# A graph, attention and product-key-memory block on one core: edge additions issued pair by pair, a shorter front, statistics taken per tile, and memory rows gathered as four slots of 32 tokens

## The chip, the cores and the metric

The kernel runs on one core of a Trainium2 chip, in one launch. The metric is the device time in microseconds, the median of the timed runs. Everything is float32.

## What is computed

For 1250 nodes of 512 features (`x`) and 20000 edges:

```python
xn = layernorm(x)
x = x + gnn(xn, src, dst, edge_type)      # two relational layers, 30 bases each
      + mix(xn)                           # two blocks: linear attention with 256 random features, then an MLP
# the memory, on y = layernorm(x):
q = (y @ Wq + bq).reshape(-1, 8, 128)     # 8 heads, two halves of 64
s1t, i1 = top_k(q1 @ keys1, 8)            # 256 keys for each half
s2t, i2 = top_k(q2 @ keys2, 8)
scores, best = top_k(s1t[:, None] + s2t[None, :], 8)
rows = i1 * 256 + i2                      # at best: 64 rows a token
out = x + sum_k relu(y . w_down[rows]) * softmax(scores) * w_up[rows]
```

The graph sum over edges is done as a product with a dense adjacency matrix (2 x 1250 x 1250 counts in DRAM).

## The kernel before

The 1250 tokens are ten tiles of 125 tokens, handled in five pairs where a stage works on 250 columns. All five engine programs are written out by hand, with semaphores between them. What stands first in a program runs first on that engine, and an engine waits in order. The stages:

1. **Front.** SP (SyncE's queue) loads `x`, the edges, then every weight of the first attention block (`attn_loads_sp`): three matrices, seven short vectors whose elements are scattered (L415), two broadcast vectors, the projection. Only then come the edge cells' way through DRAM (L303, L304, and L306, which spreads them over all partitions, 10 MB), the write of the normalised `x` (L309) and the zeroing of two adjacency copies (L314, 25 MB). DVE computes the cells, the statistics and norm of `x` (L344 to L352), and then the same statistics again for the attention block's own norm (`ln1_dve`, L445).
2. **Attention, block 0** (`attn1_*` to `attn3_*`). Beside the keys of each pair, `merge_dve` compares the edges' cells with each other, to merge repeated edges (32 of 160 groups a pair). After the last pair `edge_index_dve` makes all 160 groups' indices, and only then GpSimd (POOL) starts its 160 indirect additions into the adjacency copies (`adjacency_pool`, L285), followed by ten DMAs that add one copy to the other (L292). Behind them on POOL's queue stand the 60 loads of half a basis each for graph layer 2 (`half_bases_pool`, L1085).
3. **MLP of block 0** (`mlp_*`), opened by `ln2_dve`: statistics of all ten tiles (L829), then the norm. Beside it DVE combines the bases of graph layer 1, which SP loads (L434).
4. **Graph layers** (`gcn_*`), with the half bases combined on DVE (L1097) ahead of each tile's `xroot` addition (L1109).
5. **Attention, block 1**, and again `ln2_dve`.
6. **Memory and the second MLP** (`mem_*`), the last 1.1 ms. The MLP is cut into halves of a pair; half g runs beside tile g-3. For each tile of tokens, `front` on PE makes the queries (L1241) and scores (L1253), `top` on DVE searches them, and POOL gathers 64 times 128 rows of 4 KB (a down row and an up row) into a ring of 8 buffers (L1210), one gather for each slot: partition p holds token p. `dot` on DVE (L1538) multiplies the down half by the token and sums; ACT turns the 125 sums into a diagonal matrix of 125 x 125 (L1385); PE multiplies that matrix by the up half and adds into bank 7 (L1304). The buffer is then free, and POOL, which waits for `p_up`, may issue the next gather into it. `TURN_AT`, `QUERY_AT`, `SCORE_AT`, `HALF_AT`, `SEARCH_AT` and `TAIL_AT` say behind which slot's row each piece of other work stands in PE's, ACT's and DVE's programs. `take` (L1546) moves a finished tile out of bank 7.

The four lines of a slot:

```python
nc.gpsimd.indirect_dma_start(out=ring[s % RING], ..., in_=a["L0_ffn_rows"], in_offset=...(ap=slots_of[t % 2][:, s:s + 1], axis=0))
nc.vector.scalar_tensor_tensor(ring[s % RING][0:P, 0:DIM], ring[...], probs_of[t % 2]...[:, s:s + 1], xl[:, t % 2, :], ALU.mult, ALU.mult, accum_out=inner[:, s:s + 1])
nc.scalar.activation(diags[:, s % DRING, :], ident[0:P, 0:P], ACT.Relu, scale=inner[:, s:s + 1])
nc.tensor.matmul(psum[7][0:P, :], diags[:, s % DRING, :], ring[s % RING][0:P, DIM:ROW], start=(s == 0), stop=(s == SLOTS - 1), ...)
```

## Time and profile before

| | |
|---|---|
| median of 3 runs | 2818.54 us (2815.58 to 2827.08) |
| the profiled execution's own time | 2807.37 us |
| its span | 2805.3 us |
| busy: PE, DVE, POOL, ACT | 91%, 53%, 37%, 25% |
| memory rows: first gather issued to last `take` | 1755.8 to 2800.2 us |
| moved by DMA | 524.29 MB, 380 MB of it by POOL's queue |

The profile is one execution. A float32 matmul of the program appears as two MATMUL records. Their ends are modelled and overlap, so what a matmul costs PE is read from the distance between starts. "issue" is time in which an engine waited for nothing that the profile shows.

### The profile page before, as it was taken

How to read it: one execution, taken by the hardware profiler on the slowest of the kernel's cores; microseconds unless marked ns; L12 is line 12 of the kernel's file. 1: busy time of each engine (PE TensorE's matmuls, PEld its weight loads, DVE VectorE, ACT ScalarE, POOL GpSimd, SP SyncE). 2: the span in 40 equal slices, each digit the busy share in tenths (PEclk: the TensorE clock that was granted, in tenths of full speed). 3: DMA queues.
4: the chain of work that ended last, by engine and by line, in shares of the span. 5: the costliest groups of instructions: out<-in, count | busy, mean ns of one | idle time of the engine just before them, and what ended most of it. 6: DMA issues, size and time to landing. Idle time of an engine off the chain costs nothing.

```text
span 2805.3 us, 25699 instructions
## 1 busy us (share of the span) xinstructions
PE 2551.7 (91%) x8620; PEld 1400.3 (50%) x8620; DVE 1479.4 (53%) x3776; ACT 707.5 (25%) x1651; POOL 1042.4 (37%) x887
## 2 busy tenths in 40 slices
PE   2999979999499999999999978999989989998877
PEld 2666656765244444445656656545445445443321
DVE  4665675455376500001335634577677677677664
ACT  0346231211010011001454311333323323322322
POOL 0005877774021100000000000566656656656665
PEclk9999989999799999999999989999999999999999
DMA  8924144548776520431005000889988988989998
GB/s 283 302 67 124 3 91 111 116 91 171 189 205 186 152 58 0 130 101 55 1 1 169 1 8 8 281 309 318 334 304 317 332 311 307 336 322 337 360 354 331
DMA packets 235961, 524.29 MB, mean 187 GB/s; under 512 B 99362, under 2 KB 99737, under 8 KB 231675
## 3 DMA queue, kind: packets, MB, share of 16 engines
q0 software_dynamic: 170032, 379.99, 41.7%
q1 hardware_dynamic: 63257, 137.66, 16.2%
q10 hardware_dynamic: 2550, 5.12, 0.5%
q8 instruction: 64, 1.05, 0.2%
q14 instruction: 58, 0.48, 0.0%
HBM read 489.51 MB, written 45.34 MB: 191 GB/s over the span
## 4 chain that ended last, share of the span: by engine, by line
PE 78%; DVE 10%; DMA 5%; issue 3%; another core or an unknown queue 2%; ACT 1%; POOL 1%; SPq 0%; POOLq 0%; DVEq 0%; ACTq 0%
PE bank L1304 13%; PE bank L1056 12%; PE bank L892 5%; PE bank L903 5%; PE bank L1284 5%; PE bank L1294 4%; PE bank L1033 4%; PE bank L668 3%; PE bank L560 3%; PE bank L774 3%; PE bank L1241 3%; PE bank L567 2%; PE bank L574 2%; PE bank L1043 2%; PE bank L600 2%
## 5 line engine op out<-in xcount | busy, mean ns | idle before, releaser
L1385 ACT ACTIVATE stage<-ident,qv 125x125 f32<-125x125 f32 x640 | 246.3, 398 | 513.9 <-DVE qv L1538 184.5
L1304 PE MATMUL bank<-qv,stage 125*125 125x512 f32 x640 | 338.9, 619 | 32.9 <-ACT stage L1385 16.1
L1538 DVE SCALAR_TENSOR_TENSOR qv<-qv 125x512 f32<-125x512 f32 x320 | 238.0, 750 | 150.6 <-DMA qv<-in_L_ffn_rows,biasb 71.2
L285 POOL DMA_INDIRECT adj<-e_cnt,e_idx x80 | 164.3, 2054 | 275.7 <-issue 238.0
L1204 POOL MEMSET wreg<- 64x2048 f32 x2 | 3.6, 1801 | 688.3 <-DVE h L699 688.2
L1210 POOL DMA_INDIRECT qv<-in_L_ffn_rows,qv x160 | 162.5, 1016 | 217.6 <-issue 140.2
L1304 PEld LDWEIGHTS bank<-qv,stage 125*125 125x125 f32 x640 | 111.1, 190 | 180.9 <-issue 113.6
L1210 POOL DMA_INDIRECT qv<-in_L_ffn_rows,biasb x160 | 161.3, 1008 | 99.8 <-PE bank L1304 71.4
L285 POOL DMA_INDIRECT adj_b<-e_cnt,e_idx x80 | 174.7, 2184 | 38.9 <-issue 26.2
L1304 PE MATMUL bank<-big,stage 125*125 125x512 f32 x320 | 166.8, 617 | 12.7 <-issue 6.5
L1056 PE MATMUL bank<-big,wreg 125*125 125x512 f32 x400 | 172.0, 592 | 0.0
L1056 PE MATMUL bank<-big,qv 125*125 125x512 f32 x400 | 171.8, 592 | 0.0
L1284 PE MATMUL bank<-stage,big 128*128 128x250 f32 x640 | 162.2, 379 | 4.9 <-ACT stage L1350 4.2
L1284 PEld LDWEIGHTS bank<-stage,big 128*128 128x128 f32 x640 | 122.7, 192 | 84.5 <-issue 68.1
L1294 PE MATMUL bank<-big 128*125 128x512 f32 x320 | 161.0, 592 | 0.0
L1538 DVE SCALAR_TENSOR_TENSOR big<-big,qv 125x512 f32<-125x512 f32 x160 | 120.0, 750 | 75.8 <-DMA big<-in_L_ffn_rows,biasb 34.8
L1033 PE MATMUL bank<-qv,stage 128*125 128x512 f32 x320 | 146.2, 601 | 0.0
L1117 DVE TENSOR_TENSOR big<-bank,big 125x512 f32<-125x512 f32 x20 | 13.8, 691 | 247.3 <-PE bank L1056 247.3
L892 PE MATMUL bank<-stage,big 128*128 128x250 f32 x640 | 139.4, 378 | 1.2 <-ACT stage L924 1.2
L865 DVE SCALAR_TENSOR_TENSOR qv<-wreg,att_b,qv 128x2048 f32<-128x2048 f32 x60 | 138.4, 2347 | 2.8
L1097 DVE SCALAR_TENSOR_TENSOR qv<-stage,att_b,qv 128x1024 f32<-128x1024 f32 x90 | 109.8, 1276 | 55.4 <-DMA stage<-in_L_gnn_basis 55.4
L903 PE MATMUL bank<-big 128*125 128x512 f32 x320 | 139.0, 592 | 0.0
(224 smaller groups left out, 4211.1 us busy)
## 6 DMA issues: line engine op xcount, KB each, us to landing
wreg<-in_L_gnn_basis SPq DMA_DIRECT2D x30, 1024.0 KB
stage<-in_L_gnn_basis POOLq DMA_DIRECT2D x45, 512.0 KB, 4.4
big<-in_L_mix_W SPq DMA_DIRECT2D x4, 4096.0 KB
adj<-adj_b POOLq DMA_DIRECT2D x9, 1328.1 KB, 41.2
adj<-wreg SPq DMA_DIRECT2D x5, 2187.5 KB
adj_b<-wreg SPq DMA_DIRECT2D x5, 2187.5 KB
wreg<-adj SPq DMA_DIRECT2D x10, 1093.8 KB
qv<-adj SPq DMA_DIRECT2D x10, 1093.8 KB
```

The source lines that it names most:

```text
L285: nc.gpsimd.indirect_dma_start(out=(adj, adj_b)[g % 2], out_offset=bass.IndirectOffsetOnAxis(ap=e_idx[:, g:g + 1], axis=0), in_=e_cnt[:, g ...
L865: nc.vector.scalar_tensor_tensor(wrel[:, 0, r, :], wreg[:, n % BRING, :], att_b[:, 0, ds(i * BLOCKS + (r * BASES + n), 1)], wrel[:, 0, r, ...
L892: mm = nc.tensor.matmul(psum[F1_BANKS[n % 4]][:, 0:PT], w1_sb[:, k, 128 * n:128 * n + 128], y_t[:, k, :], start=(k == 0), stop=(k == KC - 1))
L903: mm = nc.tensor.matmul(psum[5 + j][0:P, :], act_t[:, k % HH, P * j:P * j + P], w2_sb[:, k, :], start=(k == 0), stop=(k == HC - 1))
L1033: mm = nc.tensor.matmul(psum[2 + 3 * j + r][0:P, :], gx_t[:, j, P * k:P * k + P], wrel[:, gl, r, 512 * k:512 * k + 512], start=(k == 0), s ...
L1056: mm = nc.tensor.matmul(psum[AGG_BANKS[j]][0:P, :], slabs[gl][:, j, c, :], zrel[:, c, :], start=(c == 0), stop=(c == COLT - 1))
L1210: nc.gpsimd.indirect_dma_start(out=ring[s % RING], out_offset=None, in_=a["L0_ffn_rows"], in_offset=bass.IndirectOffsetOnAxis(ap=slots_of[ ...
L1284: mm = nc.tensor.matmul(psum[F_BANKS[n % 2]][:, 0:PT], w1_sb[:, k, 128 * n:128 * n + 128], y_t[:, k, :], start=(k == 0), stop=(k == KC - 1))
L1294: mm = nc.tensor.matmul(psum[5 + j][0:P, :], act_t[:, k % HH, P * j:P * j + P], w2_sb[:, k, :], start=(k == 0), stop=(k == HC - 1))
L1304: nc.tensor.matmul(psum[7][0:P, :], diags[:, s % DRING, :], ring[s % RING][0:P, DIM:ROW], start=(s == 0), stop=(s == SLOTS - 1), skip_grou ...
L1385: nc.scalar.activation(diags[:, s % DRING, :], ident[0:P, 0:P], ACT.Relu, scale=inner[:, s:s + 1]).then_inc(p_diag, 1)
L1538: nc.vector.scalar_tensor_tensor(ring[s % RING][0:P, 0:DIM], ring[s % RING][0:P, 0:DIM], probs_of[t % 2].rearrange("p h k -> p (h k)")[:, ...
```

## The change

**Additions behind each pair.** `edge_index_dve(dve, i)` makes the indices of pair i's 32 groups right after that pair's merges (on DVE behind kmax n = 7 in pair 0, n = 3 in the others). POOL waits for a pair's indices as it comes to them, so it can start once pair 0's are there and the zeroing has ended.

**Shorter front.** The vectors and broadcasts are issued by ACT (`setup_act`) instead of SP; `bn_stats` of `x` stands ahead of the cells; the attention block's own statistics are worked out from the first norm's by three small operations instead of ten `bn_stats` and ten `bn_aggr`.

**Statistics per tile.** `ln2_dve` loses its ten `bn_stats` and `bn_aggr`; `attn3_dve` does them tile by tile, two units behind each tile's residual. This holds for both blocks.

**Rows as four slots of 32 tokens.** A gather takes, for token group g = s % 4 (32 tokens), four slots at once: partition 32e + m holds slot 4(s // 4) + e of token 32g + m. The 64 gathers a tile and their bytes stay. The diagonal matrix becomes 128 x 32 (`wsel`), and a row's matmul writes 32 partitions of bank 7, in column group g of the array. PE issues them two at a time (`late`). New work for each tile: 32 matmuls of 16 columns that spread slots and probabilities over the partitions (`spread_slots`), 4 matmuls of 512 columns and 4 ACT copies that make four replicated tokens (`spread_x`, `xrep`), and two DVE copies of 128 x 64. Scores are two matmuls of 64 rows and 256 columns into banks 3 and 4, instead of one of 128 rows and 512 columns against padded keys. Both banks are used by every head, so a head's scores wait for the search of the head before; formerly heads alternated between the banks. The ring has 9 buffers, numbered through the tiles.

```diff
         def adjacency_pool(pool):
-            pool.wait_ge(s_idx, 4)
             pool.wait_ge(s_adjz, 5 * 64)
             for g in range(GROUPS):
+                if g % CHUNK == 0:
+                    pool.wait_ge(s_idx, 4 * (g // CHUNK) + 4)
...
+        def setup_act(act):
+            attn_vectors(act, 0)
+            act.dma_start(att_b[:, 0, :], ...)
+            act.dma_start(att_b[:, 1, :], ...)
...
             if l == 0:
-                ln1_dve(dve, 0)
+                nc.vector.tensor_tensor(rs[:, 2, :], rs[:, 0, :], rs[:, 0, :], ALU.mult).then_inc(m["stat"], 1)
+                nc.vector.memset(mv[:, :, 0:1].rearrange("p t o -> p (t o)"), 0.0).then_inc(m["stat"], 1)
+                nc.vector.tensor_tensor(mv[:, :, 1], mv[:, :, 1], rs[:, 2, :], ALU.mult).then_inc(m["stat"], 1)
+                rsqrt(dve, m["stat"], 3, mv[:, :, 1], 0, TILES)
...
+                    if l == 0 and n == (3 if i else 7):
+                        edge_index_dve(dve, i)
...
+                if n >= 12 and n % 4 == 0:
+                    nc.vector.bn_stats(st6[:, T, :], h[:, T, :]).then_inc(m["ln2"], 1)
+                if n >= 13 and n % 4 == 1:
+                    nc.vector.bn_aggr(mv[:, T, :], st6[:, T, :]).then_inc(m["ln2"], 1)
...
-        QUERY_AT = [1 + hh - hh // 2 for hh in range(PKH)]
-        SCORE_AT = [10 + 3 * hh for hh in range(PKH)]
-        SEARCH_AT = SCORE_AT[0] + 3
-        TAIL_AT = SEARCH_AT + 25
+        QUERY_AT = [4 + hh - hh // 2 for hh in range(PKH)]
+        SCORE_AT = [10 + 4 * hh for hh in range(PKH)]
+        SEARCH_AT = SCORE_AT[0] + 1
+        TAIL_AT = SEARCH_AT + 4 * PKH - 1
...
             def row(t, s):
+                g = s % 4
-                pe.wait_ge(p_diag, t * SLOTS + s + 1)
-                nc.tensor.matmul(psum[7][0:P, :], diags[:, s % DRING, :], ring[s % RING][0:P, DIM:ROW], start=(s == 0), stop=(s == SLOTS - 1),
+                nc.tensor.matmul(psum[7][WIDE * g:WIDE * g + WIDE, :], wsel[:, s % DRING, :], ring[place(t, s)][:, DIM:ROW], start=(s < 4), stop=(s >= SLOTS - 4),
                                  skip_group_check=True).then_inc(p_up, 1)
...
             def late(n):
-                if n >= 0:
+                if n >= 0 and n % 2:
+                    pe.wait_ge(p_diag, n + 1)
+                    row((n - 1) // SLOTS, (n - 1) % SLOTS)
                     row(n // SLOTS, n % SLOTS)
...
             for _ in third:
                 pass
+            for _ in behind(0):
+                pass
```

`behind(t)` is the two `spread_slots` and the first two `spread_x` of a tile. For tile 0 it stands behind `third`, what is left of MLP half 2; for the others it stands at slots 52, 53, 56 and 57 of the tile before (`SPREAD_AT`). POOL's wait for a tile's slots is now for the copy out of the bank.

PE's order where the first rows start. L1284 and L1294 are the first and second product of MLP half 2, L1233 and L1241 the token's transposes and queries. Before:

```order
L1284 MATMUL bank<-stage,big 128x250 x2
L1294 MATMUL bank<-big 125x512 x6
L1233 MATMUL bank<-ident,qv 128x125 x4
L1241 MATMUL bank<-qv,wreg 128x125 x4
L1304 MATMUL bank<-qv,stage 125x512
L1241 MATMUL bank<-qv,wreg 128x125 x8
```

After (L1305, L1315 the MLP half, L1343 `spread_slots`, L1338 `spread_x`, L1325 the rows, L1251 and L1259 transposes and queries):

```order
L1305 MATMUL bank<-stage,big 128x250 x2
L1315 MATMUL bank<-big 125x512 x6
L1343 MATMUL bank<-qv,stage 32x16 x32
L1338 MATMUL bank<-qv,stage 128x512 x4
L1325 MATMUL bank<-qv,stage 32x512 x2
L1251 MATMUL bank<-ident,qv 128x125 x4
```

The spreading of tile 0's slots, which the first gather needs, has come behind the whole MLP half.

PE's order in the middle of a tile with an MLP half. Before (L1253 a head's scores):

```order
L1284 MATMUL bank<-stage,big 128x250 x2
L1304 MATMUL bank<-qv,stage 125x512
L1284 MATMUL bank<-stage,big 128x250 x2
L1304 MATMUL bank<-qv,stage 125x512
L1253 MATMUL bank<-wreg,qv 125x512
L1304 MATMUL bank<-qv,stage 125x512
L1294 MATMUL bank<-big 125x512
L1304 MATMUL bank<-qv,stage 125x512
```

After (L1273 a head's scores):

```order
L1325 MATMUL bank<-big,stage 32x512 x2
L1315 MATMUL bank<-big 125x512
L1325 MATMUL bank<-qv,stage 32x512 x2
L1305 MATMUL bank<-stage,big 128x250 x2
L1273 MATMUL bank<-wreg,qv 125x256 x2
L1315 MATMUL bank<-big 125x512
L1325 MATMUL bank<-qv,stage 32x512 x2
```

A row stood alone between two pieces; now two rows, in neighbouring column groups, stand between every two pieces.

SP's order in the front. Before:

```order
L412 DMA wreg<-in_L_mix_Wv 128x4x512
L415 DMA cols<-in_L_mix_ln_g 128x4x1
L415 DMA cols<-in_L_mix_ln_b 128x4x1
L415 DMA cols<-in_L_mix_ln_g 128x4x1
L415 DMA cols<-in_L_mix_ln_b 128x4x1
L415 DMA cols<-in_L_mix_bq 128x4x1
L415 DMA cols<-in_L_mix_bk 128x4x1
L415 DMA cols<-in_L_mix_b 128x16x1
L417 DMA biasb<-in_L_mix_bv 125x512
L417 DMA biasb<-in_L_mix_bo 125x512
L420 DMA ctx_flat<-in_L_mix_proj 128x2x64 x2
L303 DMA cells_t<-qv 128x125
```

After:

```order
L297 DMA qv<-in_edge_type 125x160
L411 DMA wreg<-in_L_mix_Wq 128x4x512
L411 DMA wreg<-in_L_mix_Wk 128x4x512
L411 DMA wreg<-in_L_mix_Wv 128x4x512
L414 DMA ctx_flat<-in_L_mix_proj 128x2x64 x2
L300 DMA cells_t<-qv 128x125
```

Seven vectors, two broadcast biases and the two broadcasts of `att` (formerly ahead of the matrices) have left SP's queue for ACT's, where they stand first.

## Rows read from the trace of the kernel before

**Rows 1.** Page, part 2: busy tenths and GB/s in 40 slices of 70 us.
```profile
PE   2999979999499999999999978999989989998877
DMA  8924144548776520431005000889988988989998
GB/s 283 302 67 124 3 91 111 116 91 171 189 205 186 152 58 0 130 101 55 1 1 169 1 8 8 281 309 318 334 304 317 332 311 307 336 322 337 360 354 331
```

**Rows 2.** Windows, `take` to `take`: tiles 0, 1, 2, 7 and 9.
```profile
core 0: us, PE busy (x) PEld busy (x) DVE busy (x) ACT busy (x) POOL busy (x), PEclk, DMA share, GB/s
1755.80:1874.60 118.80, 111.20 (x346) 58.98 (x345) 79.18 (x255) 36.05 (x91) 72.67 (x71) 0.98 0.89 314
1874.60:1978.60 104.00, 100.97 (x318) 53.42 (x318) 70.51 (x221) 33.53 (x87) 62.91 (x64) 0.99 0.88 308
1978.60:2089.00 110.40, 101.48 (x310) 52.41 (x310) 77.31 (x250) 33.19 (x85) 64.78 (x65) 0.98 0.92 329
...
2517.80:2614.20 96.40, 81.74 (x214) 32.14 (x214) 69.05 (x219) 27.48 (x73) 64.34 (x64) 0.96 0.91 331
...
2710.50:2800.20 89.70, 71.06 (x128) 18.99 (x128) 47.84 (x128) 25.14 (x63) 57.40 (x58) 1.00 0.94 358
```

**Rows 3.** Timeline of PE: rows back to back, and eight query matmuls before a row.
```profile
1964.30 1.02 PE L1304 MATMUL bank<-stage 125*125 125x512 f32 x2
1965.16 1.88 PE L1304 MATMUL bank<-big,stage 125*125 125x512 f32 x4
...
1980.33 1.95 PE L1241 MATMUL bank<-qv,wreg 128*128 128x125 f32 x16
1982.11 1.02 PE L1304 MATMUL bank<-qv,stage 125*125 125x512 f32 x2
```

**Rows 4.** Timeline of the front: cells to all partitions, nine of ten second statistics, PE's start.
```profile
35.91 0.36 SPq L306 DMA_DIRECT2D big<-cells_t  x1
...
39.71 5.42 DVE L445 BATCH_NORM_STATS2 st<-h 125x6 f32<-125x512 f32 x9
...
50.72 1.93 PE L549 MATMUL bank<-ident,stage 125*128 125x125 f32 x8 [14.53 <-DVE stage L472]
```

**Rows 5.** Timeline of POOL: first of 160 additions, the sum after the last, the fifth half basis.
```profile
214.50 2.20 POOL L285 DMA_INDIRECT adj<-e_cnt,e_idx  x1 [210.66 <-issue]
...
661.14 9.42 POOL L292 DMA_DIRECT2D adj<-adj_b  x10 [3.60 <-DMA adj_b<-e_cnt,e_idx]
...
748.58 0.72 POOL L1085 DMA_DIRECT2D stage<-in_L_gnn_basis  x1 [75.05 <-DVE qv L1097]
```

**Rows 6.** Timeline of SP: the queue's next issue after the zeroing.
```profile
160.86 0.39 SPq L408 DMA_DIRECT2D wreg<-in_L_mix_Wo  x1
```

**Rows 7.** Timeline of DVE: last pair's products of the MLP, first half basis.
```profile
675.96 0.69 DVE L847 TENSOR_TENSOR h<-bank,h 125x512 f32<-125x512 f32 x1 [18.00 <-PE bank L903]
...
745.80 7.26 DVE L1097 SCALAR_TENSOR_TENSOR qv<-stage,att_b,qv 128x1024 f32<-128x1024 f32 x6 [50.98 <-DMA stage<-in_L_gnn_basis]
```

**Rows 8.** Waits from 684 to 770 us: who waited for whom, us, times, longest.
```profile
PE bank L1043 <- DVE big L1109: 19.7, 1, 19.7
...
PE bank L1010 <- DMA stage<-xn_d: 16.9, 1, 16.9
```

**Rows 9.** Groups by line: statistics of the second norm, twice ten tiles.
```profile
L829 DVE BATCH_NORM_STATS2 st<-h 125x6 f32<-125x512 f32 x20 | 12.1, 678 | 0.2
```

**Rows 10.** Timeline where the first rows start: a head's scores, the MLP half's end, the first gather.
```profile
1742.27 1.09 PE L1253 MATMUL bank<-wreg,qv 128*125 128x512 f32 x2 [0.50 <-DVE qv L1432]
...
1761.08 5.31 PE L1294 MATMUL bank<-big 128*125 128x512 f32 x12
...
1755.83 1.05 POOL L1210 DMA_INDIRECT qv<-in_L_ffn_rows,qv  x1 [113.97 <-issue]
```

**Rows 11.** Timeline of PE: eight matmuls in four column groups of 32, then full width.
```profile
111.33 1.05 PE L580 MATMUL bank<-stage,headsel 128*32 128x250 f32 x16
112.31 1.98 PE L600 MATMUL bank<-projbd,stage 128*125 128x512 f32 x4
```

More of the change, by code:

```diff
@@ L45 @@
 SLOTS = PKH * TOPK
-RING = 8
-ROUNDS = SLOTS // RING
+RING = 9
 DRING = 8
@@ L318, in setup_dve @@
         def setup_dve(dve):
+            dve.wait_ge(s_xin, 32)
+            for t in range(TILES):
+                nc.vector.bn_stats(st6[:, t, :], h[:, t, :]).then_inc(s_ln, 1)
             dve.wait_ge(s_edge, 48)
@@ L340, in setup_dve @@
             nc.vector.tensor_copy(cell_ts[0:GROUPS - 128, 1, :], psum[0][0:GROUPS - 128, 128:128 + P]).then_inc(s_cellsb, 1)
-            dve.wait_ge(s_xin, 32)
-            for t in range(TILES):
-                nc.vector.bn_stats(st6[:, t, :], h[:, t, :]).then_inc(s_ln, 1)
             dve.wait_ge(s_ln, TILES)
@@ L699, in residual @@
                 nc.vector.tensor_tensor(h[:, T, :], h[:, T, :], b_o, ALU.add).then_inc(m["hat"], 1)
-            for n in range(UNITS + 7):
+            for n in range(UNITS + 10):
                 if n < UNITS:
@@ L827, in ln2_dve @@
             n = l * ADDS["ln2"]
-            for t in range(TILES):
-                nc.vector.bn_stats(st6[:, t, :], h[:, t, :]).then_inc(m["ln2"], 1)
-            dve.wait_ge(m["ln2"], n + TILES)
-            for t in range(TILES):
-                nc.vector.bn_aggr(mv[:, t, :], st6[:, t, :]).then_inc(m["ln2"], 1)
             dve.wait_ge(m["ln2"], n + 2 * TILES)
@@ L1202, in mem_pool @@
             pool.wait_ge(m["hat"], ADDS["hat"] + 2 + 2 * TILES)
[L1203 to L1204 removed]
             for t in range(TILES):
[L1206 removed]
+                pool.wait_ge(p_slots, 2 * t + 1)
                 for s in range(SLOTS):
@@ L1248, in front @@
                     pe.wait_ge(p_q, t * PKH + hh + 1)
-                    if hh >= 2:
-                        pe.wait_ge(p_top, t * TOPN + 4 * (hh - 1))
+                    if hh:
+                        pe.wait_ge(p_top, t * TOPN + 4 * hh)
                     elif t:
-                        pe.wait_ge(p_top, (t - 1) * TOPN + 4 * (PKH - 1 + hh))
-                    nc.tensor.matmul(psum[3 + hh % 2][0:P, :], pq_t[:, hh, :], keybd[:, hh, :], start=True, stop=True).then_inc(p_s_pe, 1)
+                        pe.wait_ge(p_xr, 4 * t)
+                    for s in range(2):
+                        rows = slice(64 * s, 64 * s + 64)
+                        mm = nc.tensor.matmul(psum[3 + s][0:P, 0:NKEYS], pq_t[rows, hh, :], keys_t[rows, hh, :], start=True, stop=True)
+                    mm.then_inc(p_s_pe, 1)
                     yield
@@ L1321, in mem_pe @@
                 pass
+            pe.wait_ge(p_sel, 2)
+            for _ in behind(0):
+                pass
             for t in range(TILES):
                 ahead = front(t + 1) if t + 1 < TILES else iter(())
+                found = behind(t + 1) if t + 1 < TILES else iter(())
                 beside = half(half_of(t)) if half_of(t) else iter(())
                 for s in range(SLOTS):
+                    if s == 0:
+                        spread_x(t, 2)
+                        spread_x(t, 3)
+                    for _ in range(SPREAD_AT.count(s)):
+                        next(found, None)
                     for _ in range((s == TURN_AT) + QUERY_AT.count(s) + SCORE_AT.count(s)):
@@ L1340, in mem_act @@
             act.wait_ge(p_w, 32)
-            for s in range(2):
-                for b in range(4):
-                    rows = slice(64 * s, 64 * s + 64)
-                    nc.scalar.activation(keybd[rows, 2 * b:2 * b + 2, NKEYS * s:NKEYS * s + NKEYS],
-                                         psum[2 + b][rows, :].rearrange("p (h m) -> p h m", h=2), ACT.Copy).then_inc(p_keysS, 1)
+            for b in range(4):
+                nc.scalar.activation(keys_t[:, 2 * b:2 * b + 2, :], psum[2 + b][:, :].rearrange("p (h m) -> p h m", h=2), ACT.Copy).then_inc(p_keysS, 1)
             def scale(i):
```

202 lines of the change are left out of this document (125 added, 77 removed).

## The prediction

> **What bounds the kernel now.** I read the page's slices first [rows 1]: PE is busy nearly throughout, so whatever shortens PE's path counts, except in two places: slices 1 and 11 (PE 2 and 4 tenths), and the last fifteen, where DMA is as full as PE. I went to each with the timeline or the waits.
>
> *Memory stage* (1755.8 to 2800.2, 1044.4 us). The windows go from one `take` to the next [rows 2]. Tile 9, with neither search nor MLP half beside it, takes 89.7 us for 64 gathers, 1.40 us each. PE has little to do there; this I take as the gathers' own pace. Tile 7 (search, no half) takes 96.4, tile 1 (a half too) 104.0, tile 2 (also `finish`, DVE's additions and statistics for the next pair) 110.4. PE's need comes from starts [rows 3]: a row of 512 columns 0.86 us, eight query matmuls 1.78. A tile with a half needs 64 x 0.86 = 55.0 for rows, 4 x 1.78 = 7.1 for queries, 8 x 0.86 = 6.9 for scores, 0.9 for transposes, and 32 pieces of 0.86, 27.5, for the half: 97.4 of tile 1's 104.0. Tile 7 needs 69.9 of 96.4. So PE bounds tiles 0 to 6, and DMA with lumps of PE and DVE the rest; busy time misleads, being modelled.
>
> *Front*: PE starts at 50.72, waiting for DVE, which takes the same statistics twice [rows 4].
>
> *Graph layer 1*: POOL starts its additions at 214.50 and the sum at 661.14 [rows 5], although the zeroing had ended by 160.86 [rows 6]. The half bases stand behind the sum: DVE waits 50.98 us for them, from 694.8 to 745.80 [rows 7], and POOL's fifth load waits for DVE [rows 5]. PE waits 19.7 for DVE, and 16.9 more for a 250 KB load that runs beside the sum [rows 8].
>
> **The change, part by part** (us against the profiled execution).
>
> *Front: -8.* Ten `bn_stats` and ten `bn_aggr` (nine of the former are 5.42) [rows 4] give way to three small operations: -6. The first statistics move ahead of the cells, and the cells no longer queue behind eleven DMAs on SP, which could give up to 6 more. Against it, DMA is full here [rows 1], and ACT's scattered elements now compete with `x` and the edges from the start. I count 2. Ends -3 and -12.
>
> *Indices beside the pairs: +1.* Six short DVE operations behind each pair; PE's turns of the next pair cover them. If not, +3.
>
> *Statistics per tile: -9.* Ten at 0.60 and ten `bn_aggr` leave the path in each block, 6.8 [rows 9]; the last tile's own stay, 0.8, and the second block gets a 125 x 512 copy (0.9) and a reduction. That is -11; I give back 2 for DVE's extra 0.7 us a tile in `attn3`. Ends -5 and -12.
>
> *Additions earlier: -34.* Start and sum move from 214.5 to about 158, now bound by the zeroing: 56 us. The half bases then land near 690. DVE, some 14 us earlier by the terms above, wants them near 681, and PE needs DVE's result only two tiles later. Both PE stalls, 16.9 + 19.7 [rows 8], should go, with 2 us of slower matmuls behind them; I leave 5 for the remaining wait. What is late next is PE itself. Ends -39 and -1 (below).
>
> *Start of the rows: +20.* Before, the first gather goes out at 1755.83, while PE works on MLP half 2 until 1766.4 [rows 10]. Now slots go through PE behind that half. Also each head's scores wait for the previous search: formerly a head took 1.09 + 0.50 = 1.59 [rows 10], set by DVE; in series it is 1.6 of search plus 0.65 to 1.09 of scores, I take 2.5, times seven heads: +6.3. PE's half ends at 1772.7, 16 spreading matmuls take 2, the DVE copy with its semaphores 0.7: first gather at 1775.4. Ends +14 and +24. Nothing hides this, since everything after goes at the gathers' pace.
>
> *Rows in column groups: -90.* The nearest row for price is the diagonal sums [rows 11]: eight matmuls of 250 columns in four groups of 32 occupy PE for 0.98 us; one after the other they would take 8 x 0.42 = 3.3, four abreast 0.83. So a pair of rows costs 0.86 at least and 1.72 at most; I take 1.0, since the overlap there was nearly full, and 32 pairs cost 32, not 55. Added: 4 x 0.86 = 3.4 (`spread_x`) and 32 small matmuls, two records each at 0.98 / 16 = 0.06, 3.9. Need with a half: 97.4 - 23 + 7.3 = 81.7, under the gathers' 89.7. Scores stay at 6.9 (3.5 if the two row halves overlap). ACT's matrix, a quarter as wide, saves perhaps 0.2 us a slot off the path. DVE keeps its 70 to 77 us and gets 0.6.
> A tile then goes at 89.7 plus the ring's stalls. Eight query pieces (14 us on PE) still fall behind five slots, and DVE's tail of the search is as thick as before, so I stay nearer to tile 7 than to tile 9: 94 for odd tiles, 98 with `finish` (4 of its 6.4, the rest in slack), 93 for tiles 7 and 8, 89.7 for tile 9, 102 for tile 0 with 4 for its first landing. 102 + 3 x 94 + 3 x 98 + 186 + 89.7 = 954, against 1044.
>
> Sum: -8 + 1 - 9 - 34 + 20 - 90 = -120. 2807.4 - 120 = 2687; the median of the runs stands 11 above the profiled execution, so 2698.
>
> **The rivals.**
>
> *A: the gathers alone set the pace.* If the ninth buffer and a faster PE leave no stall, ten tiles take 897 + 4: 53 less, 2645. For it: tile 9. Against: lumps of PE and DVE remain. 0.17.
>
> *B: changing between full width and column groups costs.* PE now changes twice for each pair. Each change may wait until the array is empty; a matmul's tail beyond its pitch is about 0.2 us (four records last 1.98, at 0.43 each 1.72) [rows 11], so 32 x 0.4 = 13 us a tile. PE needs 94.7 with a half, and such tiles come to 101 and 105: 6 x 7 + 6 = 48 more, 2746. For it: pairs stand singly between full-width pieces. Against: 0.98 for eight matmuls leaves only 0.15 for both changes. 0.17.
> The Trainium skill says in "TensorEngine Tiling (Array Packing)", Key Properties, that a change of tiling mode drains TensorE while different tiles work in parallel. The trace agrees with the second; it has no case of the first that costs more than 0.15 us.
>
> *C: the sum collides with basis loads.* The sum, from 661 before, moves into the last pair of the MLP, where SP still loads three bases of 1 MB. A 250 KB load beside the sum held PE 16.9 us [rows 8]; three loads so held are 51, and DVE's slack there is 18.0 [rows 7]: 33 back, 2731. 0.14.
> The Trainium skill's "DMA: Bandwidth & Descriptors" (Queues, rings and completion order) has each engine go round its queues packet by packet, which by itself would leave a load about half the rate. Its estimate would be some 10 us a basis, inside the slack, and 2698 would stand. The trace's load went slower than that.
>
> *D: the groups don't overlap (slower).* Then a pair costs 1.72, the rows 55 again, and PE needs 104.7 with a half; at the ratio of tiles 1 and 2 that is 111 and 118. Over the forecast: 3 x 17 + 3 x 20, 20 in tile 0, 7 in tiles 7 and 8: 138, so 2836. It decides from 1.5 us a pair, where PE's need is 97.4 again. Against it stands [rows 11]; but there the matmuls are short and four abreast. That the change does not do what it says would be this. 0.06.
>
> **How the numbers follow.** The forecast has 0.46, A 0.17, B 0.17, C 0.14, D 0.06. A measurement of this kernel tells about 0.5% from no change, 14 us. All but D are faster by more; B and C together, with a bad front, come near the bound: faster 0.92, same 0.04, slower 0.04. The range goes from below A to B and C together: 2635 to 2775.
>
> **What would show it.** Right: pairs of rows some 1.0 us apart from the next piece; `take` to `take` 93 to 98 with DMA at 340 GB/s or more; POOL's first addition near 158, and no DVE wait of tens of us for half bases; first gather about 20 us later after the search than before. Wrong: full-width spacing of 0.86 between rows of a pair (D), idle PE of 0.2 us around each pair (B), DVE waiting for basis loads around 640 (C), odd tiles at 90 (A), or PE starting later than 46.

## The result, and the profile after

The changed kernel takes **2769.4 us** (median of four runs, 2756.6 to 2790.9), the kernel before 2819.2 beside it: a ratio of 0.985, 95% interval 0.982 to 0.988. That is 50 us, where the prediction had 121, but inside its range and on its side. The profiled execution is the fastest of the four, 2756.6 (span 2754.8), 51 under before's; granted clock 0.939, before 0.974.

The slices of the changed kernel, to be read against [rows 1]:

```profile
PE   3999989997999999999999987889879879875665
POOL 0066877760111000000000000566666656666665
PEclk9999999998999999999999998999999999987856
DMA  9934145478466601440005000799999989989998
```

PE is no longer full in the last sixteen slices, and at their end its granted clock falls too. So PE no longer fills the memory stage, as predicted. Yet the stage is little shorter. Windows from one `take` to the next, in the changed kernel; first tile 0 from its first dot product, then tiles 1, 2, 8 and 9:

```profile
core 0: us, PE busy (x) PEld busy (x) DVE busy (x) ACT busy (x) POOL busy (x), PEclk, DMA share, GB/s
1737.40:1843.70 106.30, 88.29 (x396) 34.43 (x396) 77.83 (x253) 30.87 (x90) 70.30 (x70) 0.92 0.95 340
1843.70:1946.50 102.80, 89.88 (x404) 35.66 (x404) 68.89 (x224) 31.78 (x92) 63.52 (x62) 0.93 0.89 318
1946.50:2048.70 102.20, 84.85 (x396) 33.08 (x396) 76.69 (x250) 30.55 (x89) 66.43 (x66) 0.97 0.96 349
2559.80:2658.00 98.20, 66.41 (x300) 20.60 (x300) 68.06 (x220) 24.72 (x77) 66.27 (x64) 0.73 0.94 342
2658.00:2749.70 91.70, 53.64 (x128) 5.67 (x128) 47.92 (x128) 20.25 (x63) 56.38 (x58) 0.65 0.93 352
```

Against [rows 2], tile 1 lost 1.2 us and tile 2 8.2. The windows of tiles 3 to 7, cut in the same way, are 98.6, 105.0, 100.4, 104.9 and 102.2. Forecast were 94 for odd tiles, 98 for even ones, 93 for tiles 7 and 8. Tiles 1 to 8 are 4 to 9 us over their forecasts, 6.5 in the mean, whether an MLP half stands beside them (up to tile 6) or not.

The first gather goes out at 1733.0, before at 1755.8 [rows 10]; from there to the last `take` it is 1016.7 us, before 1044.4. So 28 us came from the row stage, and 23 from what lies ahead of it. Here are the changed kernel's PE at its start, POOL's first and last additions and the sum, two of DVE's three waits for a basis, and POOL's first gathers (timelines; where a line has "to", it gives minimum, median and maximum in ns and the first and last start):

```profile
41.94 1.93 PE L559 MATMUL bank<-ident,stage 125*128 125x125 f32 x8 [12.81 <-DVE stage L483]
...
L284 POOL DMA_INDIRECT adj<-e_cnt,e_idx x80: 1977/1982/3182, 156.7 to 586.2; - x80
...
595.41 9.42 POOL L291 DMA_DIRECT2D adj<-adj_b  x10 [4.36 <-DMA adj_b<-e_cnt,e_idx]
...
640.25 4.62 DVE L878 SCALAR_TENSOR_TENSOR qv<-wreg,att_b,qv 128x2048 f32<-128x2048 f32 x2 [10.86 <-DMA wreg<-in_L_gnn_basis]
654.88 4.61 DVE L878 SCALAR_TENSOR_TENSOR qv<-wreg,att_b,qv 128x2048 f32<-128x2048 f32 x2 [10.02 <-DMA wreg<-in_L_gnn_basis]
...
681.69 1.06 PE L1024 MATMUL bank<-ident,stage 125*128 125x125 f32 x4 [13.32 <-DMA stage<-xn_d]
...
686.75 7.26 DVE L1111 SCALAR_TENSOR_TENSOR qv<-stage,att_b,qv 128x1024 f32<-128x1024 f32 x6
...
L1228 POOL DMA_INDIRECT qv<-in_L_ffn_rows,qv x10: 936/937/1348, 1733.0 to 1754.0; - x10
```

PE starts 8.8 us earlier than in [rows 4]. The additions run from 156.7, and the 50.98 us wait for half bases of [rows 7] is gone. In its place DVE waits for the last three bases beside the sum, 10.9, 10.0 and 9.4 us, and PE 13.3 for the features, which stand behind the bases on SP's queue.

Who kept POOL waiting in the row stage? Its waits from 1740 us on, in the changed kernel (us in total, times, longest):

```profile
POOL qv L1228 <- issue: 87.6, 270, 1.0
POOL qv L1228 <- PE bank L1325: 85.2, 67, 3.8
POOL big L1228 <- PE bank L1325: 40.5, 26, 3.8
POOL big L1228 <- issue: 37.5, 110, 1.1
```

and of the kernel before, from 1755 on:

```profile
POOL qv L1210 <- PE bank L1304: 140.0, 154, 3.7
POOL big L1210 <- PE bank L1304: 68.4, 60, 6.4
```

With the two other regions of the ring, POOL waited 269 us for a buffer that PE had to free, and now 162; waits with no releaser in the profile ("remote") grew from 9 to 29. But a gather also costs POOL its own 1.01 to 1.03 us and, without any wait, a gap of 0.30 ("issue"). That is 1.31 us, 84 us a tile: a floor just under the 89.7 that I had taken for the transfers' pace.

### The profile page after: what moved, and what is told of

Its sections match the earlier page's. It is cut to its first block, busy times and chain, and to the rows that moved or that the text cites. A ratio compares the mean times of both kernels' runs of the same rounds, so it can differ in the third digit from the quotient of the medians.

```text
span 2754.8 us, 27581 instructions
## 1 busy us (share of the span) xinstructions
PE 2409.9 (87%) x9500; PEld 1234.4 (45%) x9500; DVE 1468.9 (53%) x3793; ACT 681.1 (25%) x1687; POOL 1036.3 (38%) x885
## 4 chain that ended last, share of the span: by engine, by line
PE 67%; DVE 13%; DMA 8%; issue 5%; POOL 3%; another core or an unknown queue 2%; ACT 1%; SPq 0%; DVEq 0%; POOLq 0%; ACTq 0%
PE bank L1070 12%; PE bank L1325 6%; PE bank L1047 5%; PE bank L905 4%; PE bank L916 4%; PE bank L1305 4%; PE bank L1315 3%; PE bank L1259 3%; PE bank L678 3%; PE bank L792 3%; PE bank L570 3%; PE bank L584 2%; PE bank L1057 2%; PE bank L577 2%; DMA qv<-in_L_ffn_rows,qv 2%
## 5 line engine op out<-in xcount | busy, mean ns | idle before, releaser
L1228 POOL DMA_INDIRECT qv<-in_L_ffn_rows,qv x356 | 360.1, 1012 | 1009.4 <-issue 909.0
L1448 ACT ACTIVATE stage<-stage,qv 128x32 f32<-128x32 f32 x640 | 200.3, 321 | 576.8 <-issue 199.0
L1325 PE MATMUL bank<-qv,stage 128*32 128x512 f32 x712 | 257.6, 699 | 91.6 <-ACT stage L1448 48.4
L1612 DVE SCALAR_TENSOR_TENSOR qv<-qv,wreg 128x512 f32<-128x512 f32 x356 | 262.8, 746 | 118.2 <-DMA qv<-in_L_ffn_rows,qv 98.0
L1305 PE MATMUL bank<-stage,big 128*128 128x250 f32 x640 | 174.2, 399 | 7.5 <-ACT stage L1407 7.5
L1228 POOL DMA_INDIRECT big<-in_L_ffn_rows,qv x142 | 145.8, 1027 | 88.1 <-PE bank L1325 40.5
L1315 PE MATMUL bank<-big 128*125 128x512 f32 x320 | 173.0, 633 | 2.1 <-issue 2.1
L1325 PE MATMUL bank<-big,stage 128*32 128x512 f32 x284 | 135.1, 722 | 35.9 <-ACT stage L1448 21.0
L1305 PEld LDWEIGHTS bank<-stage,big 128*128 128x128 f32 x640 | 115.6, 194 | 108.0 <-issue 91.1
L878 DVE SCALAR_TENSOR_TENSOR qv<-wreg,att_b,qv 128x2048 f32<-128x2048 f32 x60 | 138.4, 2348 | 32.9 <-DMA wreg<-in_L_gnn_basis 30.3
L1131 DVE TENSOR_TENSOR big<-bank,big 125x512 f32<-125x512 f32 x20 | 13.8, 692 | 247.2 <-PE bank L1070 247.2
L1612 DVE SCALAR_TENSOR_TENSOR big<-big,qv,wreg 128x512 f32<-128x512 f32 x142 | 105.4, 746 | 55.0 <-DMA big<-in_L_ffn_rows,qv 48.9
L905 PEld LDWEIGHTS bank<-stage,big 128*128 128x128 f32 x640 | 122.4, 192 | 20.1 <-issue 6.0
L1325 PEld LDWEIGHTS bank<-qv,stage 128*32 128x32 f32 x712 | 32.2, 115 | 213.3 <-ACT stage L1448 109.8
L1099 POOL DMA_DIRECT2D stage<-in_L_gnn_basis x45 | 35.8, 955 | 226.1 <-DVE qv L1111 226.1
```

The costliest lines, as they stand in the source:

```text
L878: nc.vector.scalar_tensor_tensor(wrel[:, 0, r, :], wreg[:, n % BRING, :], att_b[:, 0, ds(i * BLOCKS + (r * BASES + n), 1)], wrel[:, 0, r, ...
L905: mm = nc.tensor.matmul(psum[F1_BANKS[n % 4]][:, 0:PT], w1_sb[:, k, 128 * n:128 * n + 128], y_t[:, k, :], start=(k == 0), stop=(k == KC - 1))
L1228: nc.gpsimd.indirect_dma_start(out=ring[place(t, s)], out_offset=None, in_=a["L0_ffn_rows"], in_offset=bass.IndirectOffsetOnAxis(ap=slots_ ...
L1305: mm = nc.tensor.matmul(psum[F_BANKS[n % 2]][:, 0:PT], w1_sb[:, k, 128 * n:128 * n + 128], y_t[:, k, :], start=(k == 0), stop=(k == KC - 1))
L1315: mm = nc.tensor.matmul(psum[5 + j][0:P, :], act_t[:, k % HH, P * j:P * j + P], w2_sb[:, k, :], start=(k == 0), stop=(k == HC - 1))
L1325: nc.tensor.matmul(psum[7][WIDE * g:WIDE * g + WIDE, :], wsel[:, s % DRING, :], ring[place(t, s)][:, DIM:ROW], start=(s < 4), stop=(s >= S ...
```

## The experiments

The runs fall into five sessions, each on one chip: e1 to e4, e5 to e8, e9 to e12, e13 to e16, and e17 with e18. They went at two paces. In nine of the runs the last tile, whatever the kernel, took 82.7 to 84.0 us (first, third and fifth session, called "quick" here; before 2784 to 2788 in the median), in the others 90.1 to 91.3, about as in the profile above (before 2808 to 2819); e8 and e12, which change that tile's gathers, are placed by their before. The expectations take this for a difference between chips. That is not shown: the first three sessions, quick, not quick and quick again, carry the same chip number. So I compare within a session, or between ratios of sessions of one pace. Each ratio is to the kernel before in its own session. The diffs are shortened.

**e1, the parts ahead alone.** The edit: the memory stage and its buffers taken from the kernel before, all else from the changed one.

> The changed kernel's front, index pieces, statistics per tile and earlier additions, with the memory stage of the kernel before. In the changed kernel's profile the last pair's statistics before the memory stage end about 45 us earlier than before. Theory 1 (nearly all of the gain was made ahead of the rows, and column groups gave almost nothing): about 2774 us, 45 under the kernel before, and within 0.5% of the changed kernel's 2769. Theory 2 (the parts ahead gave less than those 45 in the median, and the column groups gave the rest): 2790 or more.

Measured: 2749.4, ratio 0.988 [0.985, 0.990], 34 us under before, in a quick session. In such sessions the changed kernel stands at 0.978 (e9, e18). So the parts ahead are worth 34 us there and the new memory stage 27. Neither theory's figure fits, both being worked out for the other pace; the split is nearer to the second.

That split belongs to the quick pace. From the first gather to the last `take` the old memory stage takes 1024.6 us in e1 and the new one 981.0 in e9, while the first gather comes 19 later (1736.5 against 1717.9): 25 net. In the two profiles compared above the same sum is 28 less 23 for the later start, 5 us. At the pace at which the forecast was made, nearly the whole 50 us came from the parts ahead.

**e2, a cheaper handover of slots.**

```diff
-    for g in range(4): for e in range(4): matmul(psum[bank][32e:32e+32, 16g:16g+16], selx[:, g, 0:32], what[:, e, :])
+    for g in range(4): matmul(psum[bank][:, 64g:64g+64], selx[:, g, :], what)     # and four copies on DVE
+    for _ in range(7): yield      # between the copy of the slots and that of the probabilities
```

> The changed kernel with a cheaper handover of the next tile's slots: four matmuls of 64 columns instead of 16 of 16 columns for each of the two spreads (with four copies on DVE), and the copy of the probabilities three slots later. In nine tiles DVE stands 29.2 us waiting to copy the probabilities and 14.3 us waiting to copy the slots. Theory 1 (these waits stop the ring and so the gathers): up to 43 us less than the changed kernel, some 2730. Theory 2 (the gathers set the pace, and a stall is made up from the rows that landed meanwhile): under 10 us less, 2760 to 2770. Theory 3 (PE sets the pace by the number of its instructions): 2750, by nine times 2 us of PE.

Measured: 0.978 [0.974, 0.982]: the changed kernel's own ratio in such sessions. Nothing gained. The waits had been read at the other pace. DVE's copy of the probabilities (nine tiles) in the changed kernel of the first profile, and in e9, quick:

```profile
L1562 DVE COPY qv<-bank x9: 223/224/225, 1826.0 to 2644.0; 128x64 f32<-128x64 f32 x9
its engine sat idle before it (us, times) until:
  remote: 29.2, 9
```

```profile
L1562 DVE COPY qv<-bank x9: 224/225/225, 1823.5 to 2617.5; 128x64 f32<-128x64 f32 x9
its engine sat idle before it (us, times) until:
  PE bank L1343: 7.1, 9
```

The same nine waits take 29.2 us in one session, with no releaser in the profile, and 7.1 in another.

**e3 and e10, the queries spread out.**

```diff
-        QUERY_AT = [4 + hh - hh // 2 for hh in range(PKH)]
+        QUERY_AT = [4, 5, 6, 7, 8, 9, 9, 10]      # and HALF_AT from slot 12
```

> The changed kernel with the eight query pieces of each tile behind slots 4 to 10 instead of 4 to 8, so that no slot but one has two of them; the MLP pieces begin one slot later. Between slots 8 and 13 a slot takes some 2.5 us, against 1.43 at the gathers' pace. Theory 1 (the ring of nine is used up by the lump of queries): 2 to 4 us a tile, some 25 us less than the changed kernel's 2769. Theory 2 (that slow stretch is a refill of the ring after the boundary of the tiles, not PE's lump): within 5 us of the changed kernel.

> The kernel with spread queries, now beside the changed kernel on one chip. Theory 1 (the lump of queries empties the ring): 2 to 3 us a tile, 15 to 30 us under the changed kernel. Theory 2 (its earlier ratio of 0.973 was the chip's quicker gathers): within 8 us of the changed kernel.

Measured: 0.973 [0.971, 0.975], then 0.9745 [0.972, 0.978] beside the changed kernel's 0.9777 [0.974, 0.981] in one session: 10 us between the medians, with intervals that overlap. At the other pace it is 0.983 (e16), against 0.982 for the changed kernel (e5, another session). At most a small gain: theory 2, nearly.

**e4, rows one at a time.**

```diff
-    if n >= 0 and n % 2:  wait for both; row(n - 1); row(n)
+    if n >= 0:            wait for one; row(n)
```

> The changed kernel with each row's matmul issued by itself, as before the change, instead of two at a time; so no two rows of different column groups stand next to each other on PE. Theory 1 (pairs overlap, 1.0 us a pair): PE's need rises by 64 x 0.86 - 32 x 1.0 = 23 us a tile with an MLP half, to some 105, and the seven such tiles come to about 110: 40 to 60 us over the changed kernel, 2810 to 2830. Theory 2 (pairs hardly overlap): within 10 us of the changed kernel. Theory 3 (freeing buffers one by one is worth more than the overlap): faster than the changed kernel.

Measured: 0.995 [0.993, 0.997], quick; 2772.1 against 2724 (e9) and 2726 (e18), other sessions of that pace: 48 us slower, theory 1. The overlap is real, and complete as far as starts show. First a pair between other work in the changed kernel, then a single row in e4 (timelines of PE):

```profile
1904.56 1.05 PE L1325 MATMUL bank<-qv,stage 128*32 128x512 f32 x4
1905.54 1.11 PE L1305 MATMUL bank<-stage,big 128*128 128x250 f32 x4
```

```profile
2300.08 1.05 PE L1325 MATMUL bank<-qv,stage 128*32 128x512 f32 x2
2301.06 2.05 PE L1259 MATMUL bank<-qv,wreg 128*128 128x125 f32 x16
```

Pair and single both take 0.98 us to the next piece.

**e5, the changed kernel in another session; e7, a ring of eight.**

```diff
-RING = 9          # five buffers in qv
+RING = 8          # four
```

> The changed kernel itself, for the tiles and the clock of TensorE on the chip on which the next three run. Theory 1 (the ratio to before is a matter of the kernels): 0.985 of before here too, and tile 9 at the gathers' pace of this chip. Theory 2 (chips differ in the gathers' pace, and the changed kernel, which is nearer to that pace, gains more on a quicker chip): where tile 9 takes some 84 us and not 91.7, a ratio of 0.975 or less.

> The changed kernel with eight buffers in the ring, as before the change, and not nine. Theory 1 (the ring runs empty at each lump, since a buffer is freed only with its pair): a buffer less costs 1.4 us at each of some four stalls of a tile, 30 to 60 us over the changed kernel. Theory 2 (the gathers' own rate sets the pace): within 10 us of it.

Measured in one session (last tile 91.1 and 90.1): 0.982 [0.980, 0.985] and 0.992 [0.990, 0.995]. One buffer less costs 21 us, between the theories (30 to 60, and under 10) and nearer to the first; yet the last tile doesn't feel it. The ring matters where the work is lumpy, not where it is even.

**e6, both edits.** Spread queries and the cheaper handover together.

> The queries of the earlier experiment spread over slots 4 to 10 together with the cheaper handover (spreads of four matmuls, probabilities copied three slots later). Theory 1 (two separate stalls, each of which stops the ring): their gains against the changed kernel add, another 15 to 30 us under the kernel with spread queries alone: ratio to before 0.963 to 0.968. Theory 2 (one stall hides behind the other, or the gathers' pace is reached): within 5 us of the kernel with spread queries alone, 0.973.

Measured in e5's session: 0.979 [0.975, 0.984], 6 us under the changed kernel and not told apart from it. The handover waits on DVE did go (in eight tiles 2 us are left at the two copies, against 28.4 at one of them in e5), and from the first dot product to the last `take` it is 1008 us in both profiles. So the time came back elsewhere in the tiles.

**e8, gathers of 125 rows.**

```diff
-    indirect_dma_start(out=ring[place(t, s)],          ... ap=slots_of[t % 2][:, s:s + 1] ...
+    indirect_dma_start(out=ring[place(t, s)][0:P, :],  ... ap=slots_of[t % 2][0:P, s:s + 1] ...
```

> The changed kernel with each gather fetching 125 rows of 4 KB and not 128, so the last three partitions' rows are left out of the result; nine small fills stand before the first gather (some 5 to 9 us, once). Theory 1 (bytes set the pace of the tiles): 2.3% less in each tile, 10 x 2 us, minus the fills: 10 to 15 us under the changed kernel. Theory 2 (stalls set it): no less than the changed kernel, by the fills slower.

Measured: 1.184 [1.179, 1.190], 567 us slower than the changed kernel beside it: neither theory. DMA packets in a hundred microseconds of the row stage (2500 to 2600), e8 and then e5:

```profile
DMA packets 17296, 21.29 MB, mean 213 GB/s; under 512 B 12056, under 2 KB 12056, under 8 KB 17292
q0 software_dynamic: 17162, 20.98, 103.1%
```

```profile
DMA packets 9521, 34.52 MB, mean 345 GB/s; under 512 B 1046, under 2 KB 1046, under 8 KB 9514
q0 software_dynamic: 9384, 34.18, 94.0%
```

Leaving out 2% of the rows cut the rate by 38% and brought a dozen times as many tiny packets: some 290 for each of the 41 gathers issued there, against 16 for each of 66. The Trainium skill's "DMA: Bandwidth & Descriptors" (Why a DMA increments its semaphore by 16 and not by 1) has a DMA use the largest number of engines up to 16 that divides the slowest dimension: five for 125 rows, sixteen for 128. The drop has the direction that this would give. But POOL's packets (queue q0) took 103% of the time of all 16 engines in e8 and 94% in e5, so no engine is seen standing idle, and the tiny packets aren't explained by it. The views don't name the engine of a packet: the cause of the drop stays open.

**e9, the changed kernel in a quick session.**

> The changed kernel once more, as the base of the three that run beside it on the same chip. So far the tile with nothing beside its rows took 91 us on two chips and 83 to 84 on a third. Theory 1 (the gathers' pace of the chip decides how much the change brings): a ratio of 0.98 to 0.985 where tile 9 takes 91 us, and under 0.98 where it takes 84.

Measured: 0.978 [0.974, 0.981], last tile 83.2. As expected, at the quick pace the change gives more, 62 us.

**e11, without the later residual loads.** The four later loads (after the one for the first pair) are left out, and the first pair's residual is added to every pair.

> The kernel with spread queries, without the four later loads of the residual (500 KB each, at the start of tiles 0, 2, 4 and 6); it adds the first pair's residual to every pair. In a trace the gathers fell from some 400 to 315 GB/s for 18 us beside such a load. Theory 1 (a load takes that from the gathers and the ring has nothing left over): 3 to 5 us for each of the four, 12 to 20 us under the kernel with spread queries, all of it in the tiles with an even number. Theory 2 (PE's and DVE's lumps set these 18 us): under 5 us in all.

Measured: 0.964 [0.962, 0.966], **26 us** under e10 in the same session, more than theory 1 had. Tile 2, first in e10, then in e11:

```profile
1938.50:2041.40 102.90, 87.14 (x398) 34.12 (x396) 76.88 (x249) 30.48 (x88) 65.92 (x66) 0.94 0.96 341
```

```profile
1938.10:2032.40 94.30, 84.12 (x396) 33.65 (x396) 76.94 (x251) 30.85 (x88) 65.24 (x66) 0.96 0.99 370
```

DVE and POOL work as before, and the tile is 8.6 us shorter; tiles 4 and 6 are 4.4 and 9.6 shorter. One of the four loads goes out before the first gather (in e10 at 1674, the gather at 1737), and tile 0 is no shorter without it: three loads make the price. Even tiles are now as short as odd ones (95.3 and 95.4 in the mean, tiles 1 to 6; in e10 102.8 and 96.3). The rate of all DMAs around such a load, 0.75 us a figure: first e3, where output and load both go out within the second figure, then e11, where the output alone goes out with the third:

```profile
GB/s 399 388 371 382 399 382 325 309 350 404 352 341 336 289 317 314 325 306 306 344 303 303 328 322 295 317 317 300 339 309 295 205 246 300 355 268 295 257 147 131
```

```profile
GB/s 410 415 399 415 415 410 399 415 412 404 396 410 399 410 429 415 371 344 279 388 361 350 333 393 251 235 355 322 306 311 306 317 306 284 306 382 415 404 399 410
```

With the load the rate falls to some 320 after 4 us and stays there; without it 400 and more hold for another 8.

**e12, gathers of half the bytes.** Each gather fetches 2 KB a row; PE adds what already lay in the other half of the buffer.

```diff
+    in_=rows if first else rows.rearrange("n (a d) -> (n a) d", a=2)     # into the buffer's first half
```

> The kernel with spread queries, with gathers of 2 KB a row and not 4 KB (from a table seen as twice as many half rows; only the first nine gathers fetch whole rows), so the rows added are stale ones: DVE, ACT and PE do all their work, DMA half. Theory 1 (the gathers bound the tiles, and the rest waits for them): tiles with an MLP half fall to PE's need, worked out in the prediction at 82 and now nearer 85 to 90, tile 9 to 64 times the 1.24 us that POOL takes for an issue, 79: 80 to 120 us under the kernel with spread queries. Theory 2 (the chain from landing over DVE, ACT and PE to the next issue, and PE's lumps, bound them): under 40 us.

Measured: 0.969 [0.967, 0.971], 13 us under e10: theory 2. Its tile 1 and tile 9:

```profile
1846.80:1940.20 93.40, 88.17 (x404) 35.86 (x404) 67.72 (x225) 31.13 (x92) 63.42 (x61) 0.93 0.60 172
2608.30:2697.30 89.00, 56.16 (x128) 5.86 (x128) 47.40 (x127) 20.25 (x63) 65.25 (x60) 0.57 0.64 183
```

DMA falls from over 0.9 to 0.6 of the time, and tile 1 by 4 us. Tile 9 gets longer, 89.0 against 83.6. No wait of POOL there exceeds 0.3 us: it issues without a pause, 1.09 us and 0.30 for each. So the issue alone, not the bytes, is a floor of 84 us a tile (1.31 each), and of 89 here.

**e13, a light search; e14, a filled clock; e15, the residual on POOL's queue; e16, their base.** All four ran in one session (last tile 91).

```diff
+    keys = 64 if t else NKEYS;  few = TOPK if t else SLOTS        # e13, in top()
+    if half_of(n // SLOTS) is None or not 11 <= n % SLOTS <= 52:  # e14, behind each pair of rows
+        2 x matmul(psum[2][:, 256:506], ident, wqf[:, 0, 0:250])
+    if s == 20 and t % 2 == 0 and t + 2 < TILES: gpsimd.dma_start(res_p, ...)      # e15, not by SP
```

> The kernel with spread queries, with DVE's search made light from tile 1 on: it looks through 64 of 256 keys of each half, and picks the index parts of 8 of the 64 slots (the others keep those of tile 0), some 13 us of DVE a tile less; PE, ACT, the gathers and all handovers stay. Theory 1 (DVE's search, and above all its tail, where DVE is busy without a gap for nine slots at 1.85 us each, stops the ring): 6 to 9 us a tile, 55 to 80 us under the kernel with spread queries; tiles 7 and 8 within 3 us of tile 9. Theory 2 (PE's clock and the handover over PE set the tiles): under 20 us in all.

> The kernel with spread queries and, behind each pair of rows that has no MLP piece beside it, two matmuls of 250 columns into a free part of PSUM, whose result nobody reads: they fill PE, so that its clock should stay granted. Now TensorE stands at 1.2 GHz for some 260 us of the row stage. Theory 1 (the lower clock lengthens the queries and the pairs, and so the tiles): half-clock stretches nearly gone, and 2 to 5 us a tile less, 20 to 50 us under the kernel with spread queries. Theory 2 (PE at half clock is still ahead of DVE and POOL): within 8 us, or slower by the filling where PE is near its bound.

> The kernel with spread queries, with the four later residual loads issued by POOL between the gathers of slots 19 and 20, so that they stand in the gathers' own queue and not in another beside it. Theory 1 (the loss is from two queues that share the engines, 18 us at three quarters of the gathers' pace): each load costs its bytes at 400 GB/s, 1.3 us, and an issue of 1 us in place of 7: 15 to 20 us less. Theory 2 (the loss is in reading the residual itself, whichever queue does it): within 5 us of the kernel with spread queries.

> The kernel with spread queries, the base of the three beside it. The ratio to before should be 0.973 to 0.975 if the chip is one of those where the last tile takes 84 us, and 0.98 where it takes 91.

Measured: base 0.983 [0.980, 0.985], 2767.3. The light search 0.987 [0.985, 0.989]: 12 us **slower**, though DVE works 9 us less in tile 1. First e16, then e13:

```profile
1857.10:1956.40 99.30, 87.14 (x404) 35.48 (x404) 69.08 (x225) 31.82 (x92) 63.20 (x62) 0.94 0.91 328
```

```profile
1858.90:1956.30 97.40, 85.87 (x404) 35.05 (x404) 60.19 (x224) 31.75 (x93) 63.36 (x61) 0.96 0.91 325
```

DVE's search doesn't set the tiles: theory 1, which I favoured, fell. Why the kernel got slower was not found; the edit also changes which rows are gathered.
The filled clock 0.987 [0.983, 0.992], 17 us slower. Its tile 9 runs at full clock and is as long as e16's, at 0.62. First e14, then e16:

```profile
2690.50:2781.70 91.20, 66.90 (x257) 26.27 (x257) 47.73 (x126) 19.93 (x62) 56.14 (x58) 1.00 0.93 350
```

```profile
2669.20:2760.30 91.10, 54.72 (x128) 5.73 (x128) 47.67 (x125) 20.07 (x63) 57.13 (x58) 0.62 0.92 351
```

So the lower clock costs nothing there. For the tiles with a search e14 can't tell, since its filling keeps PE busy for 9 us more in tile 1 (95.8 against 87.1) and for 21 and 23 more in tiles 7 and 8, and this may delay the pairs that free buffers.
The residual on POOL's queue 0.989 [0.986, 0.991], 19 us slower: neither theory. A third of it, 6.6 us, lies in tile 0: POOL makes all four loads among the gathers, SP only three. POOL's own time for such an issue is 1.23 us, 5 us in all; the rest is not explained.

**e17, a combination, and e18, its base.** Spread queries, the cheaper handover, and the residual stored so that a pair's two rows are neighbours:

```diff
+        def pair_of(i): return res_d[2*P*i:2*P*i + 2*P, :].rearrange("(p j) d -> p j d", j=2)
```

> Spread queries, the cheaper handover of slots (four matmuls a spread, probabilities copied three slots later), and the residual kept in DRAM so that a pair's two rows lie next to each other: 125 packets of 4 KB a load in place of 250 of 2 KB. Theory 1 (a residual load slows the gathers as long as its packets stand between theirs): half the packets, half the 18 us of slower gathers, 2 to 4 us in each of four even tiles, and the three edits together 25 to 35 us under the changed kernel. Theory 2 (its bytes or its place in the tile count): only the earlier two edits' gain, 5 to 12 us under the changed kernel.

> The changed kernel, the base of the combination on the same chip: a ratio to before of 0.977 where its last tile takes 84 us, 0.982 to 0.985 where it takes 91.

Measured: 0.976 [0.974, 0.978] and 0.978 [0.976, 0.979], 3 us apart in the medians: no gain that can be told. No version was found that clearly beats the changed kernel.

## Why the prediction was wrong

Point by point, in the profiled executions:

- *Front, -8*: PE starts 8.8 earlier. Right.
- *Indices +1, statistics -9*: the MLP starts at 390.27, before 404.08, 13.8 earlier; forecast were -8, +1 and half of -9, so 11.5. Between the last block's `attn3` and its MLP another 7 are gained. Right, some 5 us better than forecast.
- *Additions earlier, -34*: the aggregation of graph layer 1 starts at 803.06, before 839.98. Of these 36.9 us, 13.8 were there already, so the term gave 23. The two old stalls on PE did go; the new one of 13.3 us is what is missing. Short by 11: **rival C happened**, at a third of its price of 33. The three waits are 10.9, 10.0 and 9.4 us, and the slack of 18 us [rows 7] took the greater part. A basis of 1 MB came every 14.3 us (half the distance from 640.25 to 668.88, at which DVE goes on). The 17 us a load that C took from [rows 8] are not far from that; what C had wrong was to count all of it as waiting, when DVE works for 4.6 us on each basis: the waits are 30.3 us, not 51. The Trainium skill's "DMA: Bandwidth & Descriptors" (Queues, rings and completion order) was the source of the estimate of some 10 us, which would have left no loss; the measured 14.3 stands.
- *Start of the rows, +20*: the first tile's queries start at 1676.1, 45.8 us earlier than before, the first gather only 22.8: +23, inside the ends of +14 and +24.
- *A pair of rows, 1.0 us*: 0.98, and e4 puts 48 us on the overlap. Right; D is excluded. A single row takes 0.98 too, where a full-width one took 0.86 [rows 3], so by that difference entering and leaving the column groups costs 0.12 us together, not B's 0.4. The Trainium skill's "TensorEngine Tiling (Array Packing)" (Key Properties) has such a change drain the engine; by these rows that is the 0.12 at most.
- ***Rows in column groups, -90*: this failed.** The stage gave 28. The step is the one that reads "A tile then goes at 89.7 plus the ring's stalls", with 4 us of stalls for odd tiles, 8 for even ones and 3 for tiles 7 and 8. I took the last tile's pace for a property of the transfers, and the rest for stalls that a freer PE would mostly end. Odd tiles came to 100.6 in the mean, even ones to 104, tiles 7 and 8 to 102 and 98: 52 us over in tiles 1 to 8, with 9 in tile 0 (from its first gather) and 2 in tile 9 the whole of what is missing. The 6.4 us by which even tiles were longer than odd ones I had put down to `finish`; e11 keeps `finish`, leaves out the residual loads, and the surplus is gone. It was the loads'.

What the runs put in its place: with PE off its bound, POOL still waits for buffers, 191 us in all (162 for PE, 29 with no releaser shown), on top of an issue that takes 84 a tile. The DMA engines are occupied for 0.89 to 0.96 of each window. That a tile is held by several things at once, with nine buffers to bridge every lump, is my reading of it; no run shows the division. Taking one load away then moves the tile little: half the bytes 13 us over the whole stage, DVE's handover waits nothing (e2), or 6 not told from nothing with the queries spread too (e6), a light search nothing, a restored clock nothing in tile 9. Adding in the wrong place costs at once: a buffer less 21 us, filling on PE 17, single rows 48. Only the residual loads have a large price of their own, 26 us; the kernel before has them as well, with even tiles 5 to 6 us over odd ones in [rows 2] and e1, so they explain the stage's length rather than the missing gain. Leaving them out of the kernel before was not run.

PE's load did end as the bound: tiles 7 and 8, without an MLP half, are now hardly shorter than odd tiles with one (95.2 and 92.5 against 94 to 97 in e11). In quick sessions they are 3 and 2 us longer than with the old memory stage (94.6 and 92.1 in e9, 91.7 and 90.0 in e1), in the two first profiles 6 and 2. So the new memory stage costs in the tiles where PE was never the bound; whether by the series of scores, by the spreading of slots, which I had priced only at the start of the rows, or by the lower clock, no run separates.

What stays open: how the 10 us between the last tile and a tile with a search divide among queries, scores and handover. No run took two of them away together with the residual loads, and a ring of ten wasn't tried, for lack of room. The granted clock in the tiles with a search but no MLP half (0.73 in tile 8, before 0.96 in tile 7) is open as a cause too. Why waits without a releaser are long at one pace and short at the other, and what makes the two paces, wasn't found either.

## What to carry to other kernels

When the engine that bounds a pipelined stage is relieved, don't forecast the next stage at the pace of its emptiest tile: add up what every unit (the issuing engine with its gaps too) holds in a full tile, and where several come close to each other, expect much less than the emptiest tile promises (here 28 us of 90). A wait that is removed between units joined by a short ring can come back elsewhere (e6), so price it by a run with a buffer less, not by its length. Look for what such a stage shares with other transfers: three loads of 500 KB cost some 26 us here, about what the whole rewriting of the rows gained in a quick session.

## What was not expected of the hardware

- An indirect gather of 125 rows of 4 KB ran at 213 GB/s, one of 128 rows at 345, with 12056 against 1046 packets under 512 bytes in 100 us (e8, e5). Why is open.
- A residual load of 500 KB, over 125 partitions, costs 4 to 10 us beside the gathers (tiles 2, 4 and 6 of e10 and e11), where its bytes at 400 GB/s take 1.3. In e17, with half its packets, no gain could be told.
- POOL's issue of an indirect gather takes 1.01 us of its own with 4 KB a row, 1.09 with 2 KB (tile 9 of e12), and 0.30 between two.
- TensorE's granted clock: with the rows in column groups PE is busy for 54 of tile 9's 92 us, and its granted clock there was 0.65, before 1.00 [rows 2]: a mean between its levels of 1.2 and 2.4 GHz. In e14 tile 9 had 1.00 again and was no shorter.
- Sessions differ by 8 us in the same last tile (83 and 91), in the kernel before by 1%, and in the gain of the change (0.978 and 0.982 to 0.985). Whether the chip, its state or something else makes it is not shown.
